# Four graph layers on one core: head transfers spread over the denominator steps of layer 0, and a Relu on ScalarE as the bound of a log ratio in layer 3

## The reference, cut to what matters

```python
e = S1[rows[:, None], kidx] + S2[rows[None, :], kidx]
e = jnp.where(valid, leaky_relu(e, 0.2), 0.0)
attn = softmax(e, axis=1)
out = jnp.einsum('ijh,jhd->ihd', attn, Vh).reshape(n, h * d)
```

```python
u  = mobius_add(-x, y)                       # num / max(den, 1e-7)
un = clip(norm(u), 1e-7, 1.0 - 1e-5)
logs = 2.0 / lambda_x(x) * arctanh(un) * (u / un)
v = sum(where(mask, logs, 0.0), axis=1)
```

## Time and profile before

| | us |
|---|---|
| median of 3 runs | 1172.86 (1170.25 to 1174.24) |
| the profiled execution | 1168.28 |
| its span, first to last instruction | 1166.1 |
| PE busy | 973.7 (84%) |
| DVE busy | 761.3 (65%) |
| ACT busy | 551.9 (47%) |
| POOL busy | 530.0 (45%) |
| mean granted TensorE clock | 0.862 of 2.4 GHz |

### The profile page before, as it was taken

The page is one execution under the profiler, slowest core; times in us unless marked ns, Lnnn a source line. Parts: engine busy times, 40 slices in busy tenths (PEclk is TensorE's granted clock), DMA queues, the critical chain, the costliest instruction groups (busy, mean ns, idle before and its releaser), DMA issues.

```text
span 1166.1 us, 14519 instructions
## 1 busy us (share of the span) xinstructions
PE 973.7 (84%) x5239; PEld 343.5 (29%) x5239; DVE 761.3 (65%) x1185; ACT 551.9 (47%) x943; POOL 530.0 (45%) x658
## 2 busy tenths in 40 slices
PE   2898998989989897998998389999559499888970
PEld 1662221212112121221224332333332244444430
DVE  3326775757668575775775567311449679999987
ACT  0645664646656464664662066000100367777760
POOL 1108786868869586795881000000000045555542
PEclk8757998999989898997998589999659768998885
DMA  9640011020201102021000000000010000000000
GB/s 184 120 133 22 21 27 60 21 75 18 69 21 29 58 21 71 16 65 32 20 15 7 0 1 1 1 1 1 1 37 1 1 0 1 1 0 1 1 0 18
DMA packets 24940, 34.05 MB, mean 29 GB/s; under 512 B 16219, under 2 KB 16363, under 8 KB 23718
## 3 DMA queue, kind: packets, MB, share of 16 engines
q1 hardware_dynamic: 22566, 24.75, 7.4%
q0 software_dynamic: 2304, 8.39, 3.9%
HBM read 40.22 MB, written 1.30 MB: 36 GB/s over the span
## 4 chain that ended last, share of the span: by engine, by line
PE 58%; DVE 19%; SPq 7%; DMA 7%; issue 4%; ACT 2%; POOL 2%; DVEq 0%; POOLq 0%
PE ps L1068 15%; PE ps L1078 8%; PE ps L1175 7%; DVE big L403 4%; PE ps L1055 4%; PE ps L1047 3%; DMA den_scratch<-y_nat 3%; SPq L263 3%; SPq L266 3%; PE ps L1209 3%; PE ps L1149 3%; DVE big L399 2%; DVE big L714 2%; DVE big L400 2%; PE ps L1245 2%
## 5 line engine op out<-in xcount | busy, mean ns | idle before, releaser
L522 DVE COPY_PREDICATED big<-mask,ps 128x512 f32<-128x512 uint8 x512 | 337.3, 721 | 124.0 <-PE ps L1055 111.0
L360 POOL TENSOR_SCALAR big<-big 128x512 f32<-128x512 f32 x512 | 355.4, 711 | 122.4 <-PE ps L1078 120.7
L845 ACT ACTIVATE ps<-ps 128x512 f32<-128x512 f32 x512 | 267.6, 582 | 200.8 <-PE ps L1047 200.6
L1068 PE MATMUL ps<-big 128*64 128x512 f32 x1024 | 268.2, 632 | 0.0
L372 POOL TENSOR_TENSOR big<-big 128x512 f32<-128x512 f32 x40 | 55.1, 1377 | 354.3 <-ACT big L905 354.1
L1047 PE MATMUL ps<-op_r,op_l 18*128 18x512 bf16 x512 | 116.3, 395 | 36.7 <-DVE big L522 35.5
L1078 PE MATMUL ps<-big 128*32 128x512 f32 x1024 | 140.3, 620 | 0.0
L1068 PEld LDWEIGHTS ps<-big 128*64 128x64 f32 x1024 | 60.0, 139 | 141.1 <-issue 99.8
L1245 PE MATMUL ps<-big 66*128 66x512 f32 x160 | 91.3, 703 | 4.5 <-DVE big L399 3.1
L403 DVE TENSOR_TENSOR big<-big,mask 128x512 f32<-128x512 f32 (+1 forms) x72 | 75.0, 1061 | 11.7 <-ACT big L865 10.3
L376 POOL TENSOR_TENSOR big<-big 128x512 f32<-128x512 f32 x40 | 51.1, 1277 | 52.0 <-ACT big L913 52.0
(11 more groups left out here) (234 smaller groups left out, 1150.5 us busy)
## 6 DMA issues: line engine op xcount, KB each, us to landing
big<-max_scratch SPq DMA_DIRECT2D x9, 1024.0 KB, 5.6
big<-in_adj_dram POOLq DMA_DIRECT2D x16, 512.0 KB, 8.2
big<-rden_scratch SPq DMA_DIRECT2D x30, 256.0 KB, 3.3
op_l<-split_scratch SPq DMA_DIRECT2D x64, 36.0 KB
op_r<-split_scratch SPq DMA_DIRECT2D x64, 36.0 KB
x_nat<-in_x_dram SPq DMA_DIRECT2D x1, 512.0 KB, 4.1
out_dram<-x_nat SPq DMA_DIRECT2D x1, 512.0 KB, 3.8
den_scratch<-y_nat SPq DMA_DIRECT2D x30, 8.0 KB
```

Of the source, the lines that this page charges most:

```text
L360: pool.tensor_scalar(ring[:, k % RING, :], vrow[:, head % 2, i0:i0 + HALF], HUGE, g0[:, head, jt:jt + 1], ALU.min, ALU.max).then_inc(s["ba ...
L522: dve.copy_predicated(ring[:, k % RING, :], mask[:, jt, i0:i0 + HALF], ps[:, k % SLOTS, :])\
L845: act.activation(ps[:, k % SLOTS, :], ps[:, k % SLOTS, :], ACT.Relu, scale=-1.0).then_inc(s["relus"], 1)
L1068: m = pe.matmul(ps[w * D:(w + 1) * D, MAIN, :], vp[:, head, jt + w, :], ring[:, (u + w) % RING, :], start=(jt == 0), stop=(jt == NT - 2))
```

## The change

In layer 0 SP no longer stages a head in one go. `stage_rows(head, q)` issues one pair of the 16 operand transfers; `stage_slot(n, c)` is called three times in every denominator step (c = 0 behind the first transfer, 1 behind the second, 2 behind the fourth) and issues pair q = 3 (n mod 4) + c, and at q = 8 the row. The head is n // 4 + 1. Heads 0 and 1 are staged as before.

In layer 3 DVE's clamp goes. ACT applies a Relu with scale -1 instead, so that the tile holds the ratio's logarithm with its sign turned and bounded from below by 0; the signs of the following scales turn too. The upper bound 1 - 1e-5 comes as a factor in the two lower bounds (a second operation of the same two instructions) and in the scales of the two Ln. The lower bound LO is gone.

```diff
-            def stage_head(head):
+            def stage_rows(head, q):
...
+            def stage_slot(n, c):
+
+                head, q = n // BLOCKS + 1, n % BLOCKS * 3 + c
+                if 2 <= head < H:
+                    if q < 8:
+                        stage_rows(head, q)
+                    elif q == 8:
+                        stage_row(head)
...
                 sp.wait_ge(s["den_free"], n + 1)
                 sp.dma_start(den_d[n, :, :], den_t[0:P:32, n % 2, :]).then_inc(s["den_dma"], 16)
+                stage_slot(n, 0)
                 sp.wait_ge(s["den_dma"], 16 * (n + 1))
                 sp.dma_start(den4[:, n % 2, :, :], den_d[n, :, :].rearrange("w (p n) -> p w n", n=DR)).then_inc(s["den_in"], 16)
+                stage_slot(n, 1)
                 sp.wait_ge(s["rden_ready"], n + 1)
...
                 sp.dma_start(rrow[:, n % 2, :], rden_d[n:n + 1, :].to_broadcast([P, HALF])).then_inc(rrow_in[n % 2], 16)
-                head = n // BLOCKS
-                if n % BLOCKS == BLOCKS - 1 and head + 2 < H:
-                    stage_head(head + 2)
-                    stage_row(head + 2)
+                stage_slot(n, 2)
```

```diff
-                    ts(wA[:, u, :], ps[:, 0, :], BALL_EPS, None, ALU.max).then_inc(s["den_c"], 1)
+                    ts(wA[:, u, :], ps[:, 0, :], BALL_EPS, top, ALU.max, ALU.mult).then_inc(s["den_c"], 1)
...
-                    ts(wB[:, u, :], ps[:, 1, :], BALL_EPS, None, ALU.max)\
+                    ts(wB[:, u, :], ps[:, 1, :], BALL_EPS, 1.0 / top, ALU.max, ALU.mult)\
...
-                    dve.wait_ge(s["ratioc"], k - 1)
-                    dve.scalar_tensor_tensor(wB[:, u, :], wB[:, u, :], -0.5, wA[:, u, :], ALU.mult, ALU.subtract)\
+                    dve.scalar_tensor_tensor(wB[:, u, :], wB[:, u, :], 0.5, wA[:, u, :], ALU.mult, ALU.subtract)\
                         .then_inc(s["scl"], 1)
-                if 1 <= k <= n3:
-                    u = (k - 1) % NW
-                    dve.wait_ge(s["ratio"], k)
-                    ts(wB[:, u, :], wB[:, u, :], LO, HI, ALU.max, ALU.min).then_inc(s["ratioc"], 1)
...
+                    act.wait_ge(s["ratio"], k)
+                    act.activation(wB[:, u, :], wB[:, u, :], ACT.Relu, scale=-1.0).then_inc(s["ratioc"], 1)
                     act.wait_ge(s["ratioc"], k)
-                    act.activation(wC[:, u, :], wB[:, u, :], ACT.Exp, scale=0.5).then_inc(s["un"], 1)
+                    act.activation(wC[:, u, :], wB[:, u, :], ACT.Exp, scale=-0.5).then_inc(s["un"], 1)
```

More of the change, by code:

```diff
@@ L255, in stage_row @@
                 sp.dma_start(vrow[:, head % 2, :], m_d[head:head + 1, :].to_broadcast([P, N])).then_inc(vrow_in[head % 2], 16)
-            def stage_head(head):
[L259 to L268, removed]
+            def stage_rows(head, q):
+                b, g, w = head % 2, q // 2, q % 2
+                r0 = 32 * g + NINE * w
+                sp.dma_start(op_l[r0:r0 + NINE, b, :],
+                             split_d[(2 + w) * H + head, :, :].unsqueeze(1).to_broadcast([PARTS, PARTS, N]))\
+                    .then_inc(staged[b], 16)
+                sp.dma_start(op_r[r0:r0 + NINE, b, :],
+                             split_d[w * H + head, :, :].unsqueeze(0).to_broadcast([PARTS, PARTS, N]))\
+                    .then_inc(staged[b], 16)
+            def stage_slot(n, c):
[5 more added lines that the diff above has]
+                        stage_row(head)
             stage_row(0)
             sp.wait_ge(s["rows_out"], 16 * (NQ * PARTS * NT // P))
-            stage_head(0)
+            for q in range(8):
+                stage_rows(0, q)
             stage_row(1)
-            stage_head(1)
+            for q in range(8):
+                stage_rows(1, q)
             for n in range(BY_ROW):
@@ L690, in _ @@
                     .then_inc(s["g_read"], 1)
-            LO, HI = 2.0 * math.log(BALL_EPS), 2.0 * math.log(1.0 - 1e-5)
+            top = 1.0 - 1e-5
             for k in range(n3 + LAG_M):
@@ L907, in _ @@
                     u = (k - 1) % NW
+                    act.wait_ge(s["ratio"], k)
+                    act.activation(wB[:, u, :], wB[:, u, :], ACT.Relu, scale=-1.0).then_inc(s["ratioc"], 1)
                     act.wait_ge(s["ratioc"], k)
-                    act.activation(wC[:, u, :], wB[:, u, :], ACT.Exp, scale=0.5).then_inc(s["un"], 1)
+                    act.activation(wC[:, u, :], wB[:, u, :], ACT.Exp, scale=-0.5).then_inc(s["un"], 1)
                     act.wait_ge(s["un"], k)
-                    act.activation(wD[:, u, :], wC[:, u, :], ACT.Ln, bias=1.0).then_inc(s["l1"], 1)
+                    act.activation(wD[:, u, :], wC[:, u, :], ACT.Ln, bias=1.0, scale=1.0 - 1e-5).then_inc(s["l1"], 1)
                     act.wait_ge(s["l1"], k)
-                    act.activation(wC[:, u, :], wC[:, u, :], ACT.Ln, bias=1.0, scale=-1.0).then_inc(s["l2"], 1)
+                    act.activation(wC[:, u, :], wC[:, u, :], ACT.Ln, bias=1.0, scale=-(1.0 - 1e-5)).then_inc(s["l2"], 1)
                 if k >= 2:
```

## The result

The changed kernel takes 1211.28 us (median, 1196.63 to 1223.3) against 1173.55 us of the kernel before, measured beside it. The ratio, 1.0225 with a 95% interval of 1.0152 to 1.0299, is that of the fast runs alone, without those over 1.5% above the fastest of their kernel (1216.8 and 1223.3 of the changed kernel). The forecast was 1181, in a range that ended at 1195. So the direction was right and the size was not: +8 us were forecast on the profile's scale, and the profiled execution, the shortest of the changed kernel's, shows +28.4 (1196.63 against 1168.28). Measured once more, the changed kernel had 1215.69 us and a ratio of 1.0344 (1.0256 to 1.0432).

The account below looks back on a forecast made before the run. PE was taken to bound layer 0, with stalls at six staging bursts, and DVE layer 3. Layer 0 +20 and layer 3 -12 made +8 on 1168.28, so 1176, plus 4.6 for the median: 1181 us, range 1165 to 1195.

Parts of the forecast that it names:

- The bursts' 41.5 us of DVE: Layer 0: DVE's six waits for denominators held up by bursts of staging transfers, 41.5 us in all, would go.
- The operand waits: Layer 0: PE waits for late operands, 3.0 us in two heads and 1.1 in two; +8 us (+5 to +11).
- Rival (a): Spreading works with nothing in its place: layer 0 loses 62 us, layer 3 its 12, 1099 us; chance 0.04.
- The row's landing: Layer 0: the row's time from issue to landing behind a 256 KB broadcast, taken as 6.3 us (5.4 to 8.1).
- the term says +12: Layer 0: PE's idle time grows by 12 us (+6.5 to +23) from DVE's six waits of 8.9 us.
- The 4 us behind each stall stay as they are.: Layer 0: the low clock and refilling behind each of six stalls cost some 4 us each, unchanged.
- 4.35 us a tile: Layer 3: the distance between tiles 7 and 39 falls from 4.71 to 4.35 us.
- -12 us: Layer 3: gain over 32 tiles from moving the clamp off DVE to ACT; bounds -24 and +5.
- the 4.1 to 4.4 of the forecast: Layer 3: time per tile of ACT's seven activations, in us.
- The sum: Layers 0 and 3 together: +20 - 12 = +8 us, 1181 us as a median; chance 0.61.
- ACT alone: Layer 3: +5 us if ACT's chain comes to 4.85 us a tile with its waits.

Follow-up runs that it names:

- one_step_earlier: The changed kernel with all of layer 0's transfer slots one step earlier: 1101.91 us, ratio 0.9413 to the kernel before.
- row_ahead: The changed kernel with each head's row issued in front of the 256 KB broadcast of the same step, not behind it: 1194.08 us, ratio 1.0194.
- l3_alone: The kernel before with only the new layer 3, keeping the old order of transfers in layer 0: 1161.08 us, ratio 0.9909.
- pool_yields: The changed kernel with POOL made to wait for `add_block` before its third base tile behind normalise: 1188.09 us, ratio 1.0125.
- add_one_input: The changed kernel with `add_block` as a reduction over one operand, leaving the accumulation over heads out: 1184.38 us, ratio 1.0079.

## Why the prediction was wrong

**Right.** The bursts' 41.5 us of DVE go, all six. The row stands behind the reciprocals and the broadcast, and POOL waits for it six times. The operand waits: 3.0 us forecast for heads 2 and 5, measured 3.43 and 2.89; +8 in all, measured 10.3. Rival (a)'s price of the bursts, 62 us, was near as well: `one_step_earlier` takes 355.7 us in the steps where the forecast for it has 348.6, so 55 us go. POOL's waits for the row are up to 19.4 us and not 13, as POOL comes to the head's first tile earlier than in the kernel before (209.43 us in head 2); the row's time of landing does not depend on that.

**The row's landing, mis-sized.** 6.3 us taken, 7.2 measured, inside the bounds of 5.4 and 8.1. The argument (a broadcast ahead makes it late) was right and its size too small: I added 0.6 us for it, and `row_ahead` shows 2.3. DVE's waits are 9.5 to 9.9 in place of 8.9, and PE's idle time at the six places is 49.9 us (9.74, 7.14, 8.36, 9.64, 6.93, 8.11) against 34.9 before, so +15 where the term says +12 (+9 against the 40.7 of `l3_alone`).

**The step that failed** is the sentence "The 4 us behind each stall stay as they are." They didn't: in the block that follows, `add_block`, with two SBUF operands, stands behind POOL's whole run of base tiles in four heads or more. That is 27.1 us (463.6 - 436.5), more than all the terms that I had. With it the sum comes to 15 + 10.3 + 27.1 = 52.4, and 53.0 were measured; that it closes so well is luck, as either side moves by some 9 us from profile to profile. What the runs show is that the cost goes when POOL pauses (`pool_yields`) or when the sum is a reduction over one operand (`add_one_input`); what lets DVE in between POOL's operations in the kernel before, and not here, stays open. Half of the rule was in my hands: "An operation of DVE with its inputs in SBUF stands until POOL's is over", written for layer 3 from the earlier trace rows and not carried to layer 0, where the same two engines run side by side. But it gives the wait for one operation of POOL, some 1.2 us as in the kernel before. None of its 26 sums took more, so a wait for eight in a row could not be read there.

**Layer 3.** 4.35 us a tile was forecast and is what seven kernels with the Relu show (4.35 to 4.37), and -12 us what `l3_alone` measured (-13). The profile of the changed kernel has 4.07 and so 9 us more. In it ACT is the bound, just below the 4.1 to 4.4 of the forecast; that three engines lie within 0.3 us of each other was written down, but not that they lock into one of two rhythms. The Trainium skill's advice against relu on ScalarE ("ScalarE: Activation LUTs", "Rules for kernel authors") would have kept the clamp on VectorE; its stated ground is VectorE's speed per element in bf16, and here, in f32, the move gains 13 us, as ACT had the time and DVE had not.

**The sum.** I gave the cost behind a stall no bounds at all. The far ends of the row, the operands and ACT alone add up to +39 us, where the upper end of 1195 stands at +22 from the median before, so the range was narrower than its own terms.

## What to carry to other kernels

When an edit makes a wait longer or moves it, follow the engines through the whole next block: look for each DVE operation with two SBUF operands, and for what POOL does in that moment, since the same sum took 1.2 us beside one run of POOL and 5.5 beside another; here a wait on POOL was enough to bring it to 0.67. A transfer that is spread over other work needs a lead that is counted against its consumer: here one block of lead decided between 2 to 3% slower and 6% faster. Where several engines are within some per cent of each other in a loop, give both rhythms a price, and look at single tiles before taking a mean.

## What I had not expected of the hardware

- DVE's sum of two SBUF operands stood 5.5 us, through eight back-to-back operations of POOL; with one operand 0.66 us at the same place.
- Four extra operations on ACT (2.62 us) made the 29 distances behind them 0.28 us shorter each.
- A broadcast of 256 KB issued 0.4 us ahead of one of 1024 KB put off the landing of the second by 2.3 us.
